# Two key steps and two attends of each head group move between the query steps of a later iteration

## What is computed

```python
# stage 1: layernorm, then causal attention, 16 heads of 8 features, with a distance bias
x = x + _L0_attn_ref(_layernorm(x), W_kqv, m)
#   score = q k^T / sqrt(128) + m * (key - query), causal; softmax; times v
# stage 2: layernorm, then 6 layers of (windowed attention + gated FFN), heads of 64 features
x = x + _L0_ffn_ref(_layernorm(x), Wqkv, q_scale, k_scale, Wo, ln_g, ln_b, W1, b1, W2, b2)
```

## Time and profile before

| | |
|---|---|
| median of 3 runs | 2091.04 us (2081.29 to 2108.35) |
| the profiled execution's own time | 2092.28 us |
| its span, first to last instruction | 2089.8 us |
| mean granted TensorE clock | 0.971 of full speed |
| PE busy | 1950.5 us (93%) |
| DVE, ACT, POOL busy | 1427.0, 1190.5, 1087.3 us |
| from 60 to 300 us, PE busy in each stretch of 10 us | 8.58 to 9.91 us |
| in 13 groups from 76.83 to 296.41 us | 219.6 us |

### The profile page before, as it was taken

One profiled execution on the slowest core, in us unless ns is written; L12 is line 12 of the kernel. 1 busy time (PEld: TensorE's weight loads), 2 busy tenths in 40 slices (PEclk: granted clock), 3 DMA queues, 4 the chain that ended last, 5 costly groups with the idle time before them and its releaser, 6 DMA issues.

```text
span 2089.8 us, 104591 instructions
## 1 busy us (share of the span) xinstructions
PE 1950.5 (93%) x47704; PEld 1233.0 (59%) x47704; DVE 1427.0 (68%) x1495; ACT 1190.5 (57%) x1736; POOL 1087.3 (52%) x1017
## 2 busy tenths in 40 slices
PE   2899997999999999999999999999999999999996
PEld 1544444666666666666666666666666666666664
DVE  4453554777777677777777877777677677777773
ACT  1454645555566656565656666566656566665562
POOL 5332323455585555674556845557745458455450
PEclk9996986999999999999999999999999999999998
DMA  4000000000010000010000100000100001000000
GB/s 128 15 2 2 2 2 11 9 9 3 20 35 14 9 12 16 19 33 9 12 4 24 31 19 4 12 17 18 34 9 12 3 24 31 19 4 12 4 3 21
DMA packets 46912, 34.81 MB, mean 17 GB/s; under 512 B 12804, under 2 KB 43138, under 8 KB 46338
## 3 DMA queue, kind: packets, MB, share of 16 engines
q1 hardware_dynamic: 46466, 27.84, 5.0%
HBM read 20.49 MB, written 1.05 MB: 10 GB/s over the span
## 4 chain that ended last, share of the span: by engine, by line
PE 87%; DVE 4%; issue 3%; POOL 2%; ACT 1%; DMA 1%; SPq 0%; DVEq 0%; ACTq 0%; POOLq 0%
PE ring L607 12%; PE ring L925 11%; PE ring L832 8%; PE ring L881 8%; PE ring L609 8%; PE ring L608 8%; PE ring L933 7%; PE ring L962 3%; PE ring L857 3%; PE ring L711 3%; PE ring L874 2%; PE ring L850 2%; PE ring L654 1%; PE ring L691 1%; PE ring L939 1%
## 5 line engine op out<-in xcount | busy, mean ns | idle before, releaser
L519 POOL TENSOR_TENSOR by_cos<-by_cos,by_sin 128x512 f32<-128x512 f32 x384 | 568.5, 1502 | 119.3 <-DVE by_sin L1485 119.3
L515 POOL TENSOR_TENSOR sq_sum<-sq 128x512 f32<-128x512 f32 x192 | 245.8, 1280 | 547.8 <-ACT sq L1203 515.5
L1203 ACT ACTIVATE sq<-ring 128x1024 f32<-128x1024 f32 x192 | 196.5, 1023 | 477.2 <-PE ring L609 477.2
L1484 DVE TENSOR_TENSOR by_cos<-ring,tabs 128x1024 f32<-128x1024 f32 x192 | 234.7, 1222 | 205.9 <-ACT sq L1203 205.9
L1493 DVE SCALAR_TENSOR_TENSOR fin<-r_norm,by_cos 128x1024 f32<-128x1024 f32 x192 | 284.6, 1491 | 105.5 <-ACT r_norm L1212 59.7
L925 PEld LDWEIGHTS ring<-probs_t,v_sb 64*32 64x32 f32 x12288 | 211.1, 106 | 121.1 <-issue 120.4
L925 PE MATMUL ring<-probs_t,v_sb 64*32 64x96 f32 (+1 forms) x12288 | 272.6, 246 | 3.9 <-issue 2.2
L607 PE MATMUL ring<-parts_sb,w_hi 128*128 128x512 f32 (+1 forms) x528 | 247.9, 469 | 19.9 <-issue 6.4
L1485 DVE TENSOR_TENSOR by_sin<-ring,tabs 128x1024 f32<-128x1024 f32 x192 | 233.0, 1213 | 0.0
L1503 DVE TENSOR_REDUCE neg_max<-ring 128x8 bf16<-128x768 f32 x192 | 175.4, 959 | 60.0 <-PE ring L857 59.9
L609 PE MATMUL ring<-parts_sb,w_lo 128*128 128x512 f32 (+1 forms) x528 | 210.8, 399 | 0.0
(11 more groups left out here) (166 smaller groups left out, 3248.9 us busy)
## 6 DMA issues: line engine op xcount, KB each, us to landing
w_raw<-in_L_ffn_Wqkv SPq DMA_DIRECT2D x48, 192.0 KB, 2.8
wo_sb<-in_L_ffn_Wo SPq DMA_DIRECT2D x48, 64.0 KB, 2.0
x_in<-state SPq DMA_DIRECT2D x24, 128.0 KB, 2.4
x_in<-state SPq DMA_DIRECT2D x24, 127.8 KB, 2.7
w_raw<-in_L_ffn_W SPq DMA_DIRECT2D x6, 341.0 KB, 4.5
rot_sb<-in_rotary SPq DMA_DIRECT2D x1, 1024.0 KB
out<-x_tok SPq DMA_DIRECT2D x16, 64.0 KB, 1.6
by_cos<-in_masks SPq DMA_DIRECT2D x1, 896.0 KB
```

What stands on the lines that cost most here:

```text
L515: pool.tensor_tensor(sq_sum[:, i, :], sq[:, i, 0, :], sq[:, i, 1, :], ALU.add).then_inc(s_ss[i], 1)
L519: rot = pool.tensor_tensor(rotated[:, i, x, :], by_cos[:, i, x, :], by_sin[:, i, 1 - x, :], ALU.add)
L1484: dve.tensor_tensor(by_cos[:, i, :, :], ring[2 + i][:], tabs[:, i, 0, :, :], ALU.mult)
```

## The change

Iteration g of PE's loop now begins with four steps in turn: q0(g), k6(g-2), q1(g), k7(g-2). The attends follow later: a2(g-2) right behind them, a3(g-2) behind k0(g-1); a1(g-1) ends the iteration. So k6, k7, a2 and a3 of a group run two iterations after its q steps began. Two other things move with this. `turn_max_rows` is now followed directly by `project_group(g+1, 0)`, and `turn_group(g-2)` runs behind k2(g-1), directly ahead of `project_group(g+1, 1)`. ACT's and DVE's lists are put in the same order, and `ring_order` is rewritten so that q and k steps alternate throughout. In `EXTRA`, the number for (2, 0) goes from 77 to 79 (this line is left out below); the sum of the table goes from 104 to 106. No other matmul is added or taken away.

```diff
@@ -331,12 +331,14 @@
         O_BANK, TURN_BANK = bank[6], bank[7]
 
         def ring_order():
-            order = [(1, 0, i) for i in range(1)]
-            for g in range(GROUPS + 1):
-                by_query = [(1, g, i) for i in range(STEPS)] if g < GROUPS else []
-                by_key = [(2, g - 1, i) for i in range(STEPS)] if g > 0 else []
-                rest = by_query[1:2] + [x for i in range(6) for x in by_query[2 + i:3 + i] + by_key[i:i + 1]]
-                order += (by_query[0:1] if g > 0 else []) + rest + by_key[6:]
+            order = []
+            for g in range(GROUPS + 2):
+                for i in range(STEPS):
+                    if g < GROUPS:
+                        order.append((1, g, i))
+                    of = g - 2 if i < 2 else g - 1
+                    if 0 <= of < GROUPS:
+                        order.append((2, of, (i - 2) % STEPS))
             return order
 
         RING = ring_order()
@@ -727,33 +729,30 @@
             for g in range(GROUPS + 2):
                 s, grp = divmod(g, GROUP)
                 new, old, last = g < GROUPS, 0 < g <= GROUPS, g > 1
-                if new:
-                    scores_by_query(g, 0)
+                for i in range(2):
+                    if new:
+                        scores_by_query(g, i)
+                    if last:
+                        scores_by_key(g - 2, 6 + i)
                 if last:
-                    attend_global(g - 2, 3)
+                    attend_global(g - 2, 2)
                 if old:
                     turn_max_rows(g - 1)
-                if new:
-                    scores_by_query(g, 1)
                 if g + 1 < GROUPS:
                     project_group(g + 1, 0)
-                if new:
-                    scores_by_query(g, 2)
-                if old:
-                    scores_by_key(g - 1, 0)
-                if last:
-                    turn_group(g - 2)
-                for i in range(3, STEPS):
+                for i in range(2, STEPS):
                     if i == 5 and g + 1 < GROUPS:
                         project_group(g + 1, 1)
                     if new:
                         scores_by_query(g, i)
                     if old:
                         scores_by_key(g - 1, i - 2)
+                    if last and i == 2:
+                        attend_global(g - 2, 3)
+                    if last and i == 4:
+                        turn_group(g - 2)
                     if old and i == 5:
                         attend_global(g - 1, 0)
-                    if old and i == 7:
-                        attend_global(g - 1, 1)
                     if i == 5 and ("x", s + 1) in TURNS and grp == 1:
                         turn_x("x", s + 1)
                     if i == 5 and ("v", s + 1) in TURNS and grp == 2:
@@ -761,9 +760,7 @@
                     if i == 7 and s > 0 and grp == 2:
                         turn_x("y", s - 1)
                 if old:
-                    scores_by_key(g - 1, 6)
-                    scores_by_key(g - 1, 7)
-                    attend_global(g - 1, 2)
+                    attend_global(g - 1, 1)
             turn_x("y", SEQS - 1)
 
 
@@ -1162,10 +1159,15 @@
                 s, grp = divmod(g, GROUP)
                 old = 0 < g <= GROUPS
                 if g > 1:
-                    group_out(g - 2)
+                    exps_global(g - 2, 6)
+                    exps_global(g - 2, 7)
                 if g + 1 < GROUPS:
                     scale_group(g + 1, 0)
-                for i in range(3 if old else 0):
+                if old:
+                    exps_global(g - 1, 0)
+                if g > 1:
+                    group_out(g - 2)
+                for i in range(1, 3 if old else 1):
                     exps_global(g - 1, i)
                 if g + 1 < GROUPS:
                     scale_group(g + 1, 1)
@@ -1179,8 +1181,6 @@
                     exps_global(g - 1, i)
                 if grp == 2 and s > 0:
                     state_out(s - 1)
-                for i in range(6, 8 if old else 6):
-                    exps_global(g - 1, i)
                 if grp == 0 and s + 1 < SEQS:
                     rstd_of("x", s + 1)
                 if grp == 1 and s > 0:
@@ -1438,22 +1438,18 @@
             for g in range(GROUPS + 2):
                 s, grp = divmod(g, GROUP)
                 new = g < GROUPS
-                if new:
-                    query_max(g, 0)
+                for i in range(2 if new else 0):
+                    query_max(g, i)
                 if 0 < g <= GROUPS:
                     max_into_rows(g - 1)
-                if new:
-                    query_max(g, 1)
                 if grp == 1 and s + 1 < SEQS:
                     normalise("x", s + 1)
                 if grp == 2 and s > 0:
                     normalise("y", s - 1)
-                if new:
-                    query_max(g, 2)
+                for i in range(2, 5 if new else 2):
+                    query_max(g, i)
                 if g > 1:
                     heads_out(g - 2)
-                for i in range(3, 5 if new else 3):
-                    query_max(g, i)
                 for i in range(5, 8 if new else 5):
                     query_max(g, i)
                 if grp == 0 and s + 1 < SEQS:
```

More of the change, by code:

```diff
@@ L50 @@
 V_W = 2
-EXTRA = {(2, 0): 77, (2, 1): 1, (3, 0): 1, (3, 1): 1, (4, 0): 1, (4, 1): 1, (5, 0): 1, (5, 1): 1, (6, 0): 1, (6, 1): 1, (7, 0): 1, (7, 1): 1, (8, 0): 1, (8, 1): 1, (9, 0): 1, (9, 1): 1, (10, 0): 1, (10, 1): 1, (11, 0): 1, (11, 1): 1, (12, 0): 1, (12, 1): 1, (13, 0): 1, (13, 1): 1, (14, 0): 1, (14, 1): 1, (15, 0): 1, (15, 1): 1}
+EXTRA = {(2, 0): 79, (2, 1): 1, (3, 0): 1, (3, 1): 1, (4, 0): 1, (4, 1): 1, (5, 0): 1, (5, 1): 1, (6, 0): 1, (6, 1): 1, (7, 0): 1, (7, 1): 1, (8, 0): 1, (8, 1): 1, (9, 0): 1, (9, 1): 1, (10, 0): 1, (10, 1): 1, (11, 0): 1, (11, 1): 1, (12, 0): 1, (12, 1): 1, (13, 0): 1, (13, 1): 1, (14, 0): 1, (14, 1): 1, (15, 0): 1, (15, 1): 1}
 def rotary_constants():
```

## The result

The changed kernel takes 2198.6 us (median of 4, 2193.8 to 2206.1) against 2099.7 us (median of 4, 2081.3 to 2157.2): the ratio is 1.0505, 95% interval 1.0411 to 1.0599. It is about 100 us slower. Forecast were 2124 us and a range from 2081 to 2168; the time lies beyond it. Ratios leave out executions that lie over 1.5% above the fastest of their kernel, so that the medians of the kernel before further down (2084 to 2110 us on the several chips) stand above what the ratios compare with.

A forecast was written before the change was run, and what follows sets the result against it. PE and its clock in the first stage were taken as the bound. From the profiled 2092.3 us, 10.3 (waits, extras) + 3 (low-clock groups) + 20 (clock) gave 2125.6, less 1.2 to the median: 2124 us, range 2081 to 2168.

The forecast's parts named there:

- What bounds the kernel: First stage: PE, with 13.4 of a group's 14.82 us its own work, and its clock, whose low stretches cost about 20 us.
- Edit 1: q1 leaves the gap between turn of maxima and first projection: PE stands about 0.86 us; 14 x 0.43 = 6.0 us.
- Edit 2: `turn_group` moves directly ahead of the second projection: a 0.74 us wait replaces 0.42 us; +0.32 us in 13 iterations, 4.2 us.
- The sum of both: First-stage waits: 10.3 us at full clock, including 0.1 for two narrow extras, plus 3 us for more low-clock groups.
- a low-clock group costs up to 1.5 us more: First-stage groups at the low clock, where the two gaps had no wait before: up to 1.5 us each instead of 0.75.
- The 15.6 us of a full-clock group: Sign in the first stage: a full-clock group takes about 15.6 us; under 15 us would show the forecast wrong.
- The clock term: First stage: low-clock time of 54.6 us doubles because waits ahead of light work double, +20 us.
- the 160 us that the prediction named as a sign of being wrong: Low stretches between 63 and 303 us sum to about 110 us; under 60 or over 160 us, the forecast is wrong.
- The upper bound: First-stage clock low almost all the time: 185 us more at 0.365 us lost for each, over +67 us.
- Rival C: Clock low for most of the first stage: 120 us more low time, 2150 us and up to 2190; chance 0.25.
- The rule on transposes: Transposes don't count as clock activity, so transposes plus wait look idle for 1.4 us; makes low clock likelier, no size.
- The second stage must be unchanged: Sign: the second stage, over 80% of the span, is not touched by the change and must stay the same.

The follow-up runs named there:

- e16: Kernel before with a 256-column fp32 matmul filling its waits ahead of the first projection and of `turn_group`, warm-up 13 narrow and 8 wide: 2064.5 us, ratio 0.9884.
- e13: Changed kernel with one matmul on fp32 constants in each of the two new waits, warm-up 17 narrow and 8 wide: 2097.6 us, ratio 1.0086.
- e2: Changed kernel with the turn of maxima moved ahead of q1, k7 and a2, which removes the first new wait: 2140.4 us, ratio 1.0214.
- e3: Changed kernel with the attended group's transposes moved one pair of steps earlier, behind k1, which removes the second new wait: 2174.5 us, ratio 1.0363.
- e6: Kernel before with the attended group's transposes moved behind k2, directly ahead of the second projection (second new wait alone): 2142.4 us, ratio 1.0253.
- e15: Kernel before with 131 narrow extras in place of 77 ahead of PE's loop: 2207.2 us, ratio 1.0605; second stage 1849.9 us.
- e17: Kernel before with a warm-up of 10 wide matmuls in place of 77 narrow ones: 2183.8 us; second stage 1842.9 us.
- e1: Changed kernel with 77 narrow extras ahead of the projection of group 2 instead of 79: 2189.0 us, ratio 1.0464.
- e4: Changed kernel with both the turn of maxima and the attended group's transposes moved earlier, so neither new wait: 2128.7 us, ratio 1.0118.
- e9: Kernel before with 79 narrow extras in place of 77, nothing else: 2121.3 us, ratio 1.0246; second stage 1751.0 us.
- e12: Kernel before with three wide extras ahead of each projection and a warm-up of 15 narrow and 8 wide, same matmul count: 2089.9 us, ratio 1.0047.
- e14: Changed kernel with both transposes moved earlier, two wide extras ahead of each projection, warm-up 46 narrow and 4 wide: 2102.8 us, ratio 1.0139.

## Why the prediction was wrong

- **What bounds the kernel** held: PE with its clock, and in the first stage. One reading of it was too quick: that "the clock didn't fall because PE stood still for long, but while it ran light work" comes from windows of 1 us at the falls. Waits of 0.4 to 0.6 us end 1.4 to 2.4 us ahead of the first three falls (at 89.53, 137.22 and 163.61 us), though the same waits also stand where the clock doesn't fall. e16 has the same light work in the same places with two waits a group filled, and its clock is 1.00 from 60 to 300 us.
- **Edit 1** held: 1.44 us from turn to projection, a wait of 0.78 us (forecast 0.86). **Edit 2** held: 1.33 us, a wait of 0.68 us (forecast 0.74), and 5.79 us between the two projections (forecast 5.74). **The sum of both** held as well: by the estimate above some 11 us are left when the clock's part is taken off, where 10.3 + 3 were forecast. That a low-clock group costs up to 1.5 us more was too much; it is 24.40 - 23.34 = 1.06. The 15.6 us of a full-clock group can't be checked: no group of the changed kernel's trace lies wholly at full clock. One small wait was not foreseen: at full clock k7 waits in some groups for a maximum that DVE takes behind its statistics for the layernorm, 0.4 to 1.15 us, five times in e13.
- **The clock term failed.** "I take a doubling of the 54.6 us" was the step. In the trace the low stretches of the first stage up to the hand-over's end went from 89 to 324 us, which is 86 us instead of 20. Without the hand-over, as the 54.6 us were counted, they went to about 290 us, more than five times as much (0.58 of full clock from 57.6 to 398.8 us), far over the 160 us that the prediction named as a sign of being wrong. I had set the price of a low microsecond rightly and its direction too, but I scaled the low time with the total of the waits, as if every empty microsecond counted alike (and that total grew by 1.6 to 1.8, not by 2). e2, e3 and e6 show how steep it is: one wait less gives 58 or 24 us, and one wait of 0.7 us in each group, put in, takes 58 (269 us at the low clock in the traced execution, the longest of four). The full level, once lost, comes back only twice in the changed kernel's trace, for some 14 us from 198 us and some 20 from 293. A likely reason, not tested, is that a group at the low clock now has both waits as well, where before it had none there.
- **The upper bound was wrong too.** The bound "185 us more, 0.365 us for each, over +67" counts the low time in the length of the stage at full clock. A stage that is low throughout is longer. By the prediction's own numbers some 222 us of work at full clock take 222/0.635 = 350 us, of which nearly 300 us are more low time than before and cost about 108 us. The measured 235 us lie beyond the 185, but within this.
- **Rival C** had the right mechanism, at 0.25; even its 2150 us, and its upper end of 2190, were short. The executions agree within 12 us, with mean clocks from 0.917 to 0.926. The spread of the kernel before (2081 to 2108 us in the three runs that I had) was a sign that its clock could go either way; I used it only as noise.
- **The rule on transposes** ("TensorE: Matmul & The Clock Gate", Part 4 of the Trainium skill) isn't needed: e13 leaves all transposes where they are, fills the waits beside them and has most of the clock back. No run here tests the transposes by themselves.
- **"The second stage must be unchanged"** failed by 16.8 us in the one trace. e15 and e17 show that a stage can change by 90 us with nothing but other extras ahead of its loop. Whether the two extras did it here stays open: e1 with 77 gives 1752.2 us, e2 to e4 with 79 give 1758 to 1761, but e9 with 79 gives 1751.0 and e12, whose count is that of 77, 1757.6. The rest of the 16.8 us has no shown cause.
- Open as well is how much the new places of k6, k7, a2 and a3 cost without the waits: some 20 us by the medians of e4 and e14, with intervals of the ratio that begin at 0.9997 and 0.9987, and both have the wait for `group_out` besides.

## What to carry to other kernels

An engine whose clock follows its activity must be costed twice: a wait of 0.7 to 0.8 us in each group of 15 us was worth three to six times its own length in all, most of it by the clock (e3, e2, e6). So avoid putting a step directly behind the one whose result, through another engine, it waits for. If such a wait can't be avoided, try filling it with matmuls into a bank that is overwritten anyway, and keep the number of instructions ahead of a following loop the same while doing so. Where executions of one kernel differ by 1% or more and the granted clock differs with them, count a small loss as a possibly large one. And where a low clock lengthens the stage, count the low time in the lengthened stage.

## What the runs showed that was not expected

- Filling two waits a group (27 matmuls on constants in all) made the changed kernel 101 us faster, and its ten executions lie within 5.5 us. The same in the kernel before, with 28 narrower ones, has a ratio of 0.9884: 1.2% faster.
- 54 instructions more or 67 fewer ahead of PE's loop cost 90 to 97 us in a loop of 1750 us. It shows as waits for "issue", up to 2.6 us at one place of each pass and less at two others. Why these places, no run tells.
